# Softmax of a fused attention and expert layer: values weighed for two key blocks in a row instead of one

## What is computed

```python
scores = jnp.einsum('bhqd,bhkd->bhqk', Q, K) * (1.0 / jnp.sqrt(jnp.asarray(hs, x.dtype)))
scores = jnp.where(causal, scores, jnp.asarray(-10000000000.0, x.dtype))
att = jax.nn.softmax(scores, axis=-1)
y = jnp.einsum('bhqk,bhkd->bhqd', att, V)
...
x = x + ga * _L0_attn_ref(h, ...)
h = _layernorm(x, axis=-1) * (1 + cb) + sb
x = x + gb * _L0_ffn_ref(h, ...)
```

## Time and profile before

| what | value |
|---|---|
| median of 3 runs | 460.26 us |
| the profiled execution's own time | 458.97 us |
| its span, first to last instruction | 457.2 us |
| PE busy | 374.9 us (82%) |
| VectorE (DVE) busy | 297.0 us (65%) |
| ACT busy | 244.0 us (53%) |
| GpSimd (POOL) busy | 105.2 us (23%) |
| mean granted TensorE clock | 0.891 of full speed |

### The profile page before, as it was taken

How to read it: one execution, slowest core, us unless ns; L and a number is a source line. 1 busy time by engine, 2 the same in 40 slices (tenths; PEclk the granted TensorE clock), 3 DMA queues, 4 the chain that set the end, 5 groups by cost and what they waited for, 6 DMA issues and landing times.

```text
span 457.2 us, 7229 instructions
## 1 busy us (share of the span) xinstructions
PE 374.9 (82%) x2651; PEld 163.7 (36%) x2684; DVE 297.0 (65%) x596; ACT 244.0 (53%) x291; POOL 105.2 (23%) x149
## 2 busy tenths in 40 slices
PE   0640978978887997999989979999889798969995
PEld 0520323434324443443454434433445332213122
DVE  7372887463885869677758686786477645953332
ACT  1120002583003488687654866876547878768970
POOL 7009000024101410244324201443230023222000
PEclk9995555998556998999999979999999899989999
DMA  8014000023100026355200363553005045803540
GB/s 291 13 31 94 16 1 2 2 57 58 27 2 3 2 63 76 95 137 150 63 24 4 70 70 89 135 141 78 10 18 70 0 132 162 137 10 105 160 130 23
DMA packets 26847, 31.43 MB, mean 69 GB/s; under 512 B 6454, under 2 KB 17718, under 8 KB 26678
## 3 DMA queue, kind: packets, MB, share of 16 engines
q1 hardware_dynamic: 23740, 28.84, 27.0%
q0 software_dynamic: 3072, 2.13, 2.7%
HBM read 3.47 MB, written 1.05 MB: 10 GB/s over the span
## 4 chain that ended last, share of the span: by engine, by line
PE 56%; DVE 18%; issue 8%; ACT 8%; DMA 5%; SPq 2%; POOL 1%; ACTq 0%; DVEq 0%; POOLq 0%
PE misc L1055 21%; PE big L1055 18%; PE acc L1055 15%; DVE mx L838 7%; ACT ring L600 6%; DMA tstack<-tp 3%; PE misc L1074 2%; DVE xn L784 1%; SPq L404 1%; ACT qk_turned L608 1%; DMA q_block<-qk_turned 1%; SPq L328 1%; DVE stats L759 1%; DMA gm<-wT 1%; ACT L633 1%
## 5 line engine op out<-in xcount | busy, mean ns | idle before, releaser
L600 ACT ACTIVATE ring<-big 128x1024 f32<-128x1024 f32 (+1 forms) x224 | 198.8, 931 | 162.4 <-PE big L1055 161.1
L838 DVE TENSOR_REDUCE mx<-misc 128x1 f32<-128x512 f32 (+7 forms) x176 | 100.4, 592 | 34.2 <-PE misc L1055 30.8
L1055 PE MATMUL misc<-k_dense,q_block 128*128 128x448 bf16 (+7 forms) x250 | 76.9, 372 | 8.6 <-DVE mx L838 6.5
L1055 PE MATMUL acc<-ring,cb 128*32 128x512 f32 x512 | 68.6, 610 | 5.3 <-ACT ring L600 4.4
L1055 PE MATMUL big<-tstack,w1s 128*128 128x512 bf16 x177 | 56.3, 409 | 10.3 <-DMA tstack<-tp 5.7
L1055 PEld LDWEIGHTS misc<-k_dense,q_block 128*128 128x128 bf16 x256 | 31.3, 150 | 88.4 <-DVE mx L838 63.4
L1055 PE MATMUL big<-q_dense,k_block 128*128 128x448 bf16 (+7 forms) x248 | 54.7, 325 | 4.1 <-ACT ring L600 3.7
L1055 PE MATMUL misc<-later_key,identb 128*128 128x64 bf16 (+2 forms) x176 | 42.6, 242 | 17.5 <-DMA q_block<-qk_turned 15.4
L961 DVE SCALAR_TENSOR_TENSOR gm<-acc,cb,gm 128x512 f32<-128x512 f32 x40 | 29.9, 748 | 27.2 <-DMA gm<-wT 14.4
L1055 PEld LDWEIGHTS big<-q_dense,k_block 128*128 128x128 bf16 x256 | 31.2, 149 | 42.0 <-ACT ring L600 20.8
L1055 PE MATMUL acc<-ring,vals 128*32 128x64 f32 (+7 forms) x512 | 45.6, 429 | 0.5
(11 more groups left out here) (148 smaller groups left out, 411.1 us busy)
## 6 DMA issues: line engine op xcount, KB each, us to landing
gm<-wT SPq DMA_DIRECT2D x64, 256.0 KB
tstack<-tp SPq DMA_DIRECT2D x18, 128.0 KB, 5.4
k_dense<-qk SPq DMA_DIRECT2D x24, 64.0 KB
k_block<-qk_turned POOLq DMA_DIRECT2D x48, 32.0 KB, 3.6
q_dense<-qk SPq DMA_DIRECT2D x24, 64.0 KB
ca<-in_pack_a SPq DMA_DIRECT2D x1, 1155.0 KB, 5.3
xs<-in_x SPq DMA_DIRECT2D x4, 256.0 KB, 8.0
q_block<-qk_turned SPq DMA_DIRECT2D x32, 32.0 KB
```

The costliest lines, as they stand in the source:

```text
L600: act.activation(dst, src, func, scale=scale).then_inc(s["ring_read"], 1)
L838: dve.tensor_reduce(mx[:, g, k:k + n, blk], src, AX.X, ALU.max).then_inc(s["misc_read"], 1)
L1055: return pe.matmul(dst, lhsT, rhs, start=start, stop=stop)
```

## The change

Only PE's softmax loop is edited. Blocks are collected in `late` until there are two; then both are weighed in a row, after the scores of the block that follows. So W(0,0) and W(0,1) stand behind the scores of block 2, W(0,2) and W(0,3) behind those of block 4, and so on; W(0,6) and W(0,7) stand behind the scores of block 0 of group 1. A step of `between` keeps its place against the scores. No instruction is added or removed, and the other engines' programs are the same.

```diff
-                        if late:
-                            weigh(m, phase, *late.pop())
+                        if len(late) == 2:
+                            weigh(m, phase, *late.pop(0))
+                            weigh(m, phase, *late.pop(0))
                         late.append((g, blk))
                         if (g, blk) in between:
                             between[g, blk]()
-                weigh(m, phase, *late.pop())
+                for g, blk in late:
+                    weigh(m, phase, g, blk)
```

## The result

| what | before | after |
|---|---|---|
| median of 6 runs | 460.23 us (458.42 to 461.31) | 455.39 us (452.23 to 456.59) |
| the profiled execution's own time | 458.97 us | 453.17 us |
| its span | 457.2 us | 451.4 us |
| mean granted TensorE clock | 0.891 | 0.909 |

The ratio is 0.9888, with an interval of 0.9846 to 0.9929: 1.1% faster. The forecast was 460.0 us and no change that can be told; the range ended at 457.2 us. So it was **wrong, on the side of too little gain**.

A forecast was written before the change was run, and what follows sets the result against it. PE's order was taken to bound the kernel, PE being busy 82% of the span. Batch terms +0.2 - 0.45 - 0.8 + 0.8 = -0.25 gave 458.7 us from the profiled 458.97, or 460.0 as median; range 457.2 to 462.8.

The forecast's parts named there:

- Batches 1 and 2, up to tokens: Softmax stage up to tokens: +0.76 at norm1, -1.00 for W(1,0), about -0.4 waits, -0.15 type changes; sum -0.8 us.
- two changes fewer between bf16 and f32 products: Up to tokens in batches 1 and 2: fewer changes of product type on PE save 0.15 us.
- Batches 1 and 2, to the experts: From tokens to first Gelu: tstack lands 0.8 us earlier, table 0.3 later; gain 0.45 in batch 1, 0.8 in batch 2.
- Batch 3: Around turn_residual and to first Gelu: W(0,4) behind the wait and new waits for ACT make it 0.8 us later.
- Batch 0: Softmax stage: norm1 a little earlier, project as before, the walk ends 0.2 us later (bounds -0.2 and +0.5).
- One of my own signs of being wrong: Batch 0: the granted clock staying full throughout its second group would show the forecast wrong.
- Short waits of PE cost their own length: Softmax stages: added waits of 0.2 to 0.5 us for ACT cost only themselves, without lowering the clock.
- The clock stays up where it fell: Batch 0, before S18: the split 1.82 us wait keeps the clock up, -1.7 us; in all 456.9 to 457.5 us; chance 0.12.
- Tokens earlier brings nothing: Batches 1 and 2: DMA engines set tstack's landing whatever the issue, gain 0; 461.3 us; chance 0.20.
- The clock falls in the longer waits: Before norm1 and turn_residual: 1.7 us per fall; batch 3 alone 461.7 (0.08), all three 465.1 (0.10, shared with swinging rule).
- My point from which it decides: Clock falls once a wait reaches batch 0's 1.82 us: batch 3's about 2 us does, the 1.4 before norm1 doesn't.

The follow-up runs named there:

- pairs in batches 1 and 2: Against the kernel before: two weighs in a row in batches 1 and 2 only, one block at a time elsewhere; 455.74 us, ratio 0.9900.
- tokens ahead: Against the kernel before: old order, but in batches 1 and 2 tokens moved ahead of W(1,0); 455.21 us, ratio 0.9892.
- pairs there alone: Against the kernel before: two weighs in a row in batch 3 only, one block at a time elsewhere; 459.00 us, ratio 0.9988.
- second profile: The changed kernel run once more, nothing altered, against the kernel before; 454.86 us, ratio 0.9893.
- tokens behind: The change, but in batches 1 and 2 W(1,0) alone ahead of tokens, W(1,1) alone behind block 2's scores; 458.03 us, ratio 0.9983 to the kernel before.

## Why the prediction was wrong

**The sum, term by term.**

- *Batches 1 and 2, up to tokens* (-0.8): right in kind. From the output transposes to tokens it took 19.14 us before and 18.09 after in batch 1, -1.05. In batch 2 it took 19.57 and 20.11, +0.54, since the clock fell behind norm1; in the kernel with pairs in batches 1 and 2, where it did not, 18.52. The wait before norm1 came as foreseen in batch 1 (1.61 us against about 1.4; project 0.65 later against 0.76, by 1.82 and 2.47 us from norm1). In batch 2 it was 1.84 us, since it had been 0.78 before and not batch 1's 0.53, which I had used for both. The -0.15 for "two changes fewer between bf16 and f32 products" had no row behind it. Its size is about right and its reason is not: the trace shows 0.09 us at each way into and out of a weigh, also between two f32 products (see the last section).
- *Batches 1 and 2, to the experts* (-0.45 and -0.8): **this is the term that failed most, by its size.** The whole of each batch, from output transposes to output transposes, gave -1.23 and -0.99 in the changed kernel, and -2.56 for batch 2 with pairs where the clock did not fall behind norm1. I took tstack's landing 0.8 earlier by the issue alone, with 1.3 as a bound. It came 1.9 us earlier in batch 1, by 1.05 of earlier tokens and 0.83 of a shorter way. I let the last exp be 0.3 later; in batch 1 it was not later at all (30.44 us from the output transposes to the table load, before and after). And I costed the experts at the clock that they had had. Three errors of one sign: in batch 1 the first Gelu came 0.9 us earlier, and behind it, up to the next maxima's transposes (230.99 and 226.14), 0.36 were gained at the full clock. The kernel with tokens ahead shows batch 2 undisturbed: from output transposes to output transposes 89.49 us against 92.00, -2.5, where my bound was -1.35 (-1.39 by its own rows: 271.28 - 269.89). In the changed kernel the first Gelu of batch 2 is only 0.2 us earlier, for its table is late by the fall behind norm1; the rest of its -0.99 is gained behind it.
- *Batch 3* (+0.8): the wait before turn_residual was 2.22 us, as said, but the table load came 0.34 later and not 0.8. Too dear up to there; behind it I priced nothing, and the changed kernel won 0.95 us from the table load to the output transposes (9.57 against 10.52), where the clock held and had fallen before. So the profile shows -0.6 in place of +0.8. By the kernel with pairs there alone the effect can't be told from nothing.
- *Batch 0* (+0.2): **the second term that failed.** From the first copy to the end of the stage it was -1.55. The walk of waits was not wrong there (S18's wait is 1.31 us, as I wrote); what it lacked was the clock, which I had only in a rival. One of my own signs of being wrong came true here: batch 0 ran at the full clock throughout its second group.
- *Short waits of PE cost their own length*: right. In the changed kernel waits of 0.22 and 0.26 us stand at 92.40 and 94.11 us, and the granted clock from 92 to 96 is 1.00, as before. The Trainium skill's section that spoke against it (TensorE: Matmul & The Clock Gate, "A second HAM failure mode: psum-queue depth-cycling") is not borne out by these waits.

**The rivals.** *The clock stays up where it fell* named the mechanism and the side, and at 457.5 and 456.9 us, with a chance of 0.12, still gave too little: it took the experts at the full clock as a trimming of 0.6 us. *Tokens earlier brings nothing* is refuted by both kernels that move it alone. *The clock falls in the longer waits* is true in one place (a fall behind turn_residual came once in four, and no more often than with the old order): in batch 2 the wait before norm1, at 1.84 us, is followed by 0.5 in the changed kernel, in its second profile and in that with tokens behind, and not in the one with pairs in batches 1 and 2; with the old order's 0.78 us it never is, in nine profiles. It gives back 1.5 us (-0.99 for batch 2 where pairs without the fall have -2.56 and tokens ahead has -2.51), near the 1.7 that I priced. My point from which it decides was wrong, though: I set it between 1.70 and 1.82 us by two rows, and over thirteen profiles there is no such point, only a share of executions that fall. In batch 1, 1.61 us never did it, in three profiles.

**The step that failed, in one sentence:** the sum was made of waits at fixed durations of the instructions, while the same two waits that the change shortens, for ACT in batch 0 and for tstack in batches 1 and 2, were those behind which PE ran its next work at half speed. So +0.2 us was -1.55, and -0.45 and -0.8 were -1.2 and, where nothing else fell, -2.5; of the latter about half is that clock and half a landing that came earlier than its issue.

**What stays open.** Why the clock fell once in five with one and the same order in batch 0. Why the parts (0.5% and 1.0%) don't add up to more than 1.1% in the change: batch 2's fall is one cause that the profiles show, but the intervals are too wide to say that it is all. Whether the q_block transfers are what delays tstack. And whether pairs in batch 3 keep the clock up at its experts, as they did in four profiles of four.

## What to carry to other kernels

Before summing waits, mark in the stretches where the granted clock is below full speed and what PE waited for ahead of each: a wait there is worth its length plus the slow work behind it, which here was as much again. Move the one step that a long transfer hangs on ahead of work nobody waits for, and try that alone before reordering everything around it. And where PE looks busy at half the clock beside another engine that is also busy, test with unused products in its waits whether it is busy only because it is slow.

## What the runs showed of the hardware

- Adding useless products made the kernel faster: 8 in one wait by 0.35%, 11 in each of two waits by 0.6%, one behind each maxima unit by a further 1.6% (0.9700 against 0.9858). The Trainium skill, TensorE: Matmul & The Clock Gate, Part 1, says that a low clock is the state at rest and that activity lifts it; the stretches agree, 0.50 before and 0.93 to 1.00 with the added work.
- The clock is no function of the program alone. Behind S18's wait of batch 0 the same order of PE held 1.00 in four profiles and fell in a fifth (0.57 from 100 to 104 us), with the wait the same to 0.03 us (1.31 to 1.34), and the rise from the half clock in batch 0 came at 77.7 us in one profile of the changed kernel and at 78.3 in the other, and with the old order anywhere from 77.9 to 81.3. A single profile can't price such a place.
- A transfer's way to its consumer was 9.70 to 10.26 us when it was issued 2.0 us ahead of another engine's transfers, and 10.56 to 11.44 when it was 0.8 us ahead, in 26 cases.
- Going into or out of a weigh costs PE 0.09 us at the full clock. In the changed kernel a mask product of 64 columns is followed after 0.03 us by a score product, and after 0.12 us by a weigh:

```profile
94.33 0.19 PE L1055 MATMUL big<-earlier_query,identb 128*128 128x64 bf16 x1
94.36 0.36 PE L1055 MATMUL big<-q_dense,k_block 128*128 128x384 bf16 x1
94.56 0.19 PE L1055 MATMUL big<-earlier_query,identb 128*128 128x64 bf16 x1
94.68 1.82 PE L1055 MATMUL acc<-ring,vals 128*32 128x512 f32 x16
```

  The change of type is not the reason, though a weigh is f32 and the scores are bf16. The same mask product is followed after 0.03 us by an f32 product of the full width too (`misc<-rot,cb`, `misc<-ident,y`), and from the last f32 product of a weigh of 512 columns to the f32 product of tokens it is 0.52 us, against 0.43 to the next group of four inside a weigh. A weigh runs its products in fours, each on 32 columns of the array (128*32); whether that is the reason no run tests.
